# A gated cross-attention block on one core: seven block products folded onto one shared PSUM bank, and the row transposes of the feed-forward input spread over three attention units

## The reference

```
x  = x + tanh(g_xattn) * attention(layernorm(x), ctx)      # ctx: 8 x 750 x 1024
x  = x + tanh(g_ffn)   * ffn(layernorm(x))
attention: q = x Wq^T; k, v = ctx Wk^T, ctx Wv^T; 32 heads of 32; q and k rms-normalised;
           softmax(q k^T / sqrt(32)) v
ffn:       x1 = x Q(w1)^T; x2 = x Q(w2)^T; hidden = sigmoid(x1) * x2; out = hidden Q(w3)^T
Q(w):      clip(round(w / mean|w|), -1, 1)                 # 2816 x 1024, ternary
```

## Time and profile before

| what | value |
|---|---|
| three executions | 2386.88, 2387.74 (median), 2391.3 us |
| the profiled execution | 2394.38 us, its span 2392.6 us, mean granted clock 0.978 |
| busy, share of the span | PE 95%, PEld 55%, DVE 69%, ACT 60%, POOL 46% |
| one transpose into xT | 229 KB (112 rows of 1024 16-bit values; block 3 half of that) |
| one load of wraw | 2 transfers of 512 KB |

### The profile page before, as it was taken

How to read it: one execution, slowest core, us unless ns; L and a number is a source line. 1 busy time by engine, 2 the same in 40 slices (tenths; PEclk the granted TensorE clock), 3 DMA queues, 4 the chain that set the end, 5 groups by cost and what they waited for, 6 DMA issues and landing times.

```text
span 2392.6 us, 45650 instructions
## 1 busy us (share of the span) xinstructions
PE 2272.0 (95%) x16761; PEld 1313.5 (55%) x16786; DVE 1644.5 (69%) x2531; ACT 1427.2 (60%) x2931; POOL 1091.2 (46%) x993
## 2 busy tenths in 40 slices
PE   7998999999999999999999999878799999999999
PEld 6874566556656656556555566544344454444444
DVE  6776677786786877877877877677878666642220
ACT  5875788888888888888888888762222223221010
POOL 4674355674765756665765756642312222210000
PEclk9998999999999999999999999969899999999999
DMA  8885545545445546444545534668786454444331
GB/s 294 288 304 166 145 108 116 111 115 125 98 112 118 108 108 132 105 100 119 130 101 111 122 93 95 135 137 199 197 198 184 146 173 138 145 132 163 126 126 53
DMA packets 441328, 339.47 MB, mean 142 GB/s; under 512 B 366992, under 2 KB 388496, under 8 KB 440592
## 3 DMA queue, kind: packets, MB, share of 16 engines
q1 hardware_dynamic: 441104, 336.53, 53.9%
HBM read 184.68 MB, written 73.92 MB: 108 GB/s over the span
## 4 chain that ended last, share of the span: by engine, by line
POOL 35%; issue 28%; PE 21%; DMA 7%; DVE 6%; SPq 2%; ACT 1%; POOLq 0%; DVEq 0%; ACTq 0%
POOL krs L763 14%; PE ps L1682 11%; PE ps L1543 10%; DMA wraw<-in_wffn 5%; POOL oinv L781 5%; POOL kms L758 4%; POOL qrs L725 4%; DVE w12q L1277 2%; POOL osum L779 2%; DVE wneg L1275 2%; POOL osum L786 2%; SPq L487 1%; POOL oinv L783 1%; POOL ca L793 1%; DMA w12q<-w_ternary 1%
## 5 line engine op out<-in xcount | busy, mean ns | idle before, releaser
L1604 PE MATMUL ps<-wk,cpair 128*128 128x512 f16 x4608 | 1123.6, 381 | 18.4 <-DVE cpair L1190 10.6
L1394 DVE TENSOR_TENSOR plo<-pf,phi 125x448 f16<-125x448 f32 x768 | 570.6, 746 | 156.9 <-ACT phi L1029 154.7
L1604 PEld LDWEIGHTS ps<-wk,cpair 128*128 128x128 f16 x4608 | 395.2, 97 | 399.8 <-issue 14.1
L1038 ACT ACTIVATE pf<-ps 125x448 f32<-125x448 f32 x768 | 418.1, 544 | 141.8 <-PE ps L1624 135.3
L1029 ACT ACTIVATE phi<-pf 125x448 f16<-125x448 f32 x768 | 446.0, 581 | 8.9
L763 POOL TENSOR_TENSOR krs<-kms,mhalf 125x8 f32<-125x8 f32 x192 | 338.9, 1765 | 15.1
L758 POOL TENSOR_TENSOR kms<-kss,keps 125x8 f32<-125x8 f32 x192 | 95.3, 496 | 507.6 <-DVE kss L1360 507.6
L1648 PE MATMUL ps<-val,phi 125*128 125x65 f16 x3072 | 282.5, 193 | 41.2 <-DVE plo L1394 40.6
L1543 PE MATMUL ps<-xT,wT 128*128 128x448 f16 x1408 | 284.5, 356 | 14.3 <-DVE wT L1312 14.3
L1624 PEld LDWEIGHTS ps<-qT,kst 128*125 128x125 f16 x1536 | 212.1, 141 | 146.0 <-issue 1.8
L1624 PE MATMUL ps<-qT,kst 128*125 128x224 f16 x1536 | 280.6, 265 | 0.0
(11 more groups left out here) (120 smaller groups left out, 2848.8 us busy)
## 6 DMA issues: line engine op xcount, KB each, us to landing
gbuf<-in_wffn SPq DMA_DIRECT2D x66, 512.0 KB, 4.3
wraw<-in_wffn SPq DMA_DIRECT2D x66, 512.0 KB, 5.5
cstream<-in_ctx SPq DMA_DIRECT2D x48, 500.0 KB, 5.6
craw<-in_ctx SPq DMA_DIRECT2D x48, 500.0 KB, 4.5
hidden<-hf SPq DMA_DIRECT2D x88, 224.0 KB, 2.5
hraw<-hidden SPq DMA_DIRECT2D x14, 1408.0 KB, 6.5
q_stacked<-qnat SPq DMA_DIRECT2D x28, 512.0 KB, 3.6
w_ternary<-w12q SPq DMA_DIRECT2D x22, 512.0 KB, 3.0
```

What stands on the lines that cost most here:

```text
L1038: act.activation(pf[0:KW, e % 6, :], bank(3 + e % 3)[0:KW, 0:2 * S], ACT.Exp, bias=LN128, scale=SCALE).then_inc(p_ready, 1)
L1394: dve.tensor_tensor(plo[0:KW, e % 6, :, 0:S], pf[0:KW, e % 6, :].rearrange("p (t n) -> p t n", t=2), phi[0:KW, e % 6, :, 0:S], ALU.subtrac ...
L1604: mm = pe.matmul(bank(pt)[:, :], cpair[:, n % RING, a, kc, :], wkp[g][:, w, kc, :], start=(kc == 0 and m == 0), stop=(kc == KC - 1 and m = ...
```

## The change

Four groups of edits. (1) Phase C: the order of products becomes P1, P5, P6, P3, P7, P2, P4. P1, P6, P7 and P4 accumulate in bank 0, P5 and P3 in bank 1, P2 has bank 2. ScalarE copies the running sums out after P1, P5, P6 and P7 (`keep`: four instead of three), c21 is read by the second sigmoid straight from bank 0, c12 and c11 are the only additions of VectorE, and GpSimd makes c22 as one addition and the second half's gated product. (2) `wraw` gets a third slot; `load_w(n + 3)` stands first in SP's part of superpiece n, and `load_w(2)` right after the end of phase B. (3) 28 of the transposes into `xT` run in units 29 to 31, two or three behind each of four places in SP's order; the tail keeps the last four. Blocks 2 and 3 of a batch's rows are written in the first unit of batch b + 2 (before: in the last unit of batch b + 1), and saved there (`cn_save(4 * b - 6)`, `cn_save(4 * b - 5)`). (4) VectorE's wait for `q_saved` and the clearing of `knat` move behind the first `kss` sum.

```
         LN_STATS, LN_RSTD, LN_NORM = (4, 5), (5, 6), (6, 7)
-        LN_HIGH, LN_LOW = (6, 9, 13, 15), (7, 11, 14, 17)
-        LN_COMB = (8, 12)
+        LN_HIGH, LN_LOW = (6, 9, 18, 20), (7, 10, 19, 21)
+        LN_COMB = (8, 11)
...
-        def x_early(u, part):
-
-            if u == U - 1:
-                return {0: range(0, 4), 1: range(4, 8), 2: range(8, 12)}[part]
-            return range(12, 16) if u == U else ()
-
-        P1, P5, P7, P6, P2, P3, P4 = range(1, 8)
-        T1, T3, T2, T4 = range(1, 5)
+        X_EARLY = {U - 3: ((0, 0), (1, 0)), U - 2: ((2, 0), (3, 0), (0, 1)), U - 1: ((1, 1), (2, 1))}
+
+        def x_early(u, slot):
+
+            return [(4 * slot + q, part) for q, part in X_EARLY.get(u, ())]
+
+        P1, P5, P6, P3, P7, P2, P4 = range(1, 8)
+        T1, T2, T3, T4 = range(1, 5)
+        KEPT = ((P1, 0), (P5, 1), (P6, 0), (P7, 0))
...
-                s = j % 2
-                wait(sp, wquant_ready, 2 * (j - 1))
+                s = j % 3
+                wait(sp, wquant_ready, 2 * (j - 2))
...
                         turn_k(u - 1, 5)
+                        if u in X_EARLY:
+                            sp.wait_ge(kv_ready, KT * u)
+                        early_rows(u, 0)
...
-                        if g == G - 1 and b >= 1:
-                            cn_save(4 * b - 2)
-                        if u == U - 1:
-                            sp.wait_ge(kv_ready, KT * (U - 1))
-                        for ld in x_early(u, 0):
-                            turn_x(ld, (0, 1) if ld % 4 < 3 else (0,))
+                        early_rows(u, 1)
                         turn_k(u, 1)
-                        for ld in x_early(u, 1):
-                            turn_x(ld, (0, 1) if ld % 4 < 3 else (0,))
                         for m in gates_of_unit[1:-1]:
                             load_gates(m)
+                        early_rows(u, 2)
+                        if g == 0 and b >= 2:
+                            cn_save(4 * b - 6)
                         turn_k(u, 2)
                         load_gates(gates_of_unit[-1])
-                        for ld in x_early(u, 2):
-                            turn_x(ld, (0, 1) if ld % 4 < 3 else (0,))
+                        early_rows(u, 3)
                         if g == 1 and b >= 1:
                             x1_save(2 * b - 2)
                             x1_save(2 * b - 1)
                         turn_k(u, 3)
                         if g == 2 and b >= 1:
                             cn_save(4 * b - 3)
-                        if g == G - 1 and b >= 1:
-                            cn_save(4 * b - 1)
+                        if g == 0 and b >= 2:
+                            cn_save(4 * b - 5)
...
                     for bb in range(B // 2):
                         turn_x(4 * bb + 3, (1,))
                     load_w(1)
-                    for ld in x_early(U, 0):
-                        turn_x(ld, (0, 1) if ld % 4 < 3 else (0,))
+                    cn_save(4 * B - 6)
+                    cn_save(4 * B - 5)
...
             phase_b_over(sp)
+            load_w(2)
             x1_save(NL - 2)
             x1_save(NL - 1)
...
             for n in range(FJ):
+                if n + 3 < FJ:
+                    load_w(n + 3)
                 if n:
                     for half in range(2):
                         save_hid(n - 1, half)
                 if n + 1 < FJ:
                     save_w12(n + 1)
-                if n + 2 < FJ:
-                    load_w(n + 2)
                 if n - 1 in LATE_LOW:
                     cn_save(4 * B - 4 + LATE_LOW.index(n - 1))
                     later.append(4 * B - 4 + LATE_LOW.index(n - 1))
                 if later:
                     turn_x(later.pop(0))
...
-            def superpiece(n):
-
-                pool.wait_ge(prod_copied, 3 * n + 3)
-                wait(pool, c22_ready, n)
-                pool.tensor_tensor(s57[:, :], prod[:, n % 2, 1, :], prod[:, n % 2, 2, :], ALU.add).then_inc(s57_ready, 1)
-                pool.wait_ge(u2_ready, n + 1)
-                pool.wait_ge(s57_ready, n + 1)
-                wait(pool, hf_ready, 2 * n)
-                pool.tensor_tensor(c22[:, :], u2[:, n % 2, :], s57[:, :], ALU.add).then_inc(c22_ready, 1)
+            def gated(n):
+
+                pool.wait_ge(sg_ready[1], n + 1)
+                pool.wait_ge(c22_ready, n + 1)
+                pool.tensor_tensor(hf[:, n % 2, 1, :], hf[:, n % 2, 1, :], sg[:, 1, :], ALU.mult
+                                   ).then_inc(hf_ready[1], 1)
+
+            def sums(n):
+
+                pool.wait_ge(kept_ready, 4 * n + 4)
+                if n >= 2:
+                    pool.wait_ge(hid_saved[n % 2], 32 * (n // 2))
+                pool.tensor_tensor(hf[:, n % 2, 1, :], kept[:, n % 2, 3, :], kept[:, n % 2, 1, :], ALU.add
+                                   ).then_inc(c22_ready, 1)
...
             def gate(n, half):
 
-                b0 = 4 * (n % 2)
+                wait(act, hf_ready[half], n)
                 if half == 0:
-                    act.wait_ge(h_ready, product(n, P2))
-                    wait(act, hf_ready, 2 * n - 1)
+                    act.wait_ge(c11_ready, n + 1)
                 else:
-                    act.wait_ge(c21_ready, n + 1)
-                    wait(act, hf_ready, 2 * n)
-                act.activation(sg[:, half, :], bank(b0)[:, 0:CW] if half == 0 else c21[:, :], ACT.Sigmoid
-                               ).then_inc(sg_ready, 1)
+                    act.wait_ge(h_ready, product(n, P4))
+                act.activation(sg[:, half, :], c11[:, n % 2, :] if half == 0 else bank(4 * (n % 2))[:, 0:CW], ACT.Sigmoid
+                               ).then_inc(sg_ready[half], 1)
...
-            def keep_product(n, i):
-
-                act.wait_ge(h_ready, product(n, (P1, P5, P7)[i]))
+            def keep(n, i):
+
+                act.wait_ge(h_ready, product(n, KEPT[i][0]))
                 if n >= 2:
-                    act.wait_ge(u2_ready, n - 1)
-                    act.wait_ge(s57_ready, n - 1)
-                act.activation(prod[:, n % 2, i, :], bank(4 * (n % 2) + i)[:, 0:CW], ACT.Copy).then_inc(prod_copied, 1)
+                    act.wait_ge((c11_ready, c22_ready, c12_ready, c22_ready)[i], n - 1)
+                act.activation(kept[:, n % 2, i, :], bank(4 * (n % 2) + KEPT[i][1])[:, 0:CW], ACT.Copy).then_inc(kept_ready, 1)
 
             for n in range(NSP):
-                keep_product(n, 0)
-                keep_product(n, 1)
-                keep_product(n, 2)
-                gate(n, 0)
+                keep(n, 0)
+                if n:
+                    gate(n - 1, 0)
+                for i in range(1, 4):
+                    keep(n, i)
                 gate(n, 1)
                 if n in LATE_LOW:
                     ln_high(B - 1, LATE_LOW.index(n))
                 if n in EARLY_SPLIT:
                     hidden_high(0, EARLY_SPLIT.index(n))
+            gate(NSP - 1, 0)
...
             w_tables(0)
-            for c in range(2):
-                dve.wait_ge(q_saved[c], 16 * NT)
-            dve.memset(knat[:, :, :, :, :], 0.0).then_inc(knat_clear, 1)
+
+            def clear_knat():
+                for c in range(2):
+                    dve.wait_ge(q_saved[c], 16 * NT)
+                dve.memset(knat[:, :, :, :, :], 0.0).then_inc(knat_clear, 1)
...
                         dve.tensor_reduce(kss[0:KW, :], ksq[0:KW, :, :], AX_X, ALU.add).then_inc(kss_ready, 1)
+                        if Tb == 0:
+                            clear_knat()
...
+                dve.wait_ge(sg_ready[0], n + 1)
+                dve.wait_ge(c12_ready, n + 1)
+                dve.tensor_tensor(hf[:, n % 2, 0, :], hf[:, n % 2, 0, :], sg[:, 0, :], ALU.mult
+                                  ).then_inc(hf_ready[0], 1)
+
...
             for n in range(NSP):
-                b0 = 4 * (n % 2)
-                if n:
-                    second_half(n - 1)
                 if n + 1 < FJ:
                     quantise(n + 1, 0)
+                if n:
+                    gated(n - 1)
+                if n + 1 < FJ:
                     quantise(n + 1, 1)
                 if n >= FJ:
                     quantise_w3(n - FJ)
-                dve.wait_ge(h_ready, product(n, P6))
-                dve.wait_ge(prod_copied, 3 * n + 1)
-                if n >= 2:
-                    dve.wait_ge(c22_ready, n - 1)
...
+                wait(pe, sg_ready[1], n - 1)
                 block_product(n, 0, 0, w[:, 0, 0:4, :], True)
                 pe.wait_ge(t_ready, combo(n, T1))
                 wait(pe, c12_ready, n - 1)
                 block_product(n, 1, 2, t[:, 0, :, :], True)
-                pe.wait_ge(t_ready, combo(n, T3))
-                wait(pe, c21_ready, n - 1)
-                block_product(n, 2, 4, t[:, 1, :, :], True)
                 pe.wait_ge(t_ready, combo(n, T2))
-                wait(pe, u2_ready, n - 1)
-                block_product(n, 3, 6, t[:, 2, :, :], True)
```

(38 more changed lines are left out.)

59 lines of the change are left out of this document (27 added, 32 removed).

## The result

The changed kernel takes **2364.2 us** (median of 4 runs, 2360.1 to 2367.8) against 2387.3 (4 runs): ratio 0.990, 95% interval 0.988 to 0.992, 23 us less. Forecast were 2353.7 us and 34 less. The sign and the kind of gain held; a third of the gain is missing.

What follows compares the result with a forecast made beforehand. TensorE was taken to bound the attention, a load-quantise-save loop through a two-slot buffer the first pass. Terms -33 - 3 - 5.5 - 20 + 1.5 + 31 - 5 = -34 us gave 2353.7 us from 2387.7, range 2322 to 2374.

Steps and rivals of the forecast that it cites:

- first pass: First pass of gate and up products: third slot and earlier load end the wait for wraw; -33 us, to 246.
- second pass: Second pass of gate and up products: shorter first superpiece and smaller stalls after the early split; -3 us.
- start of the attention: Second context tile made before VectorE's wait and clearing, so TensorE gets it earlier; -5.5 us.
- blocks out of g = 3: Last unit of each batch: without GpSimd's low part holding VectorE up, 3.4 us go in six units; -20 us.
- crowding at the end of g = 2: Attention, end of units with g = 2: the moved first blocks crowd GpSimd; +1.5 us.
- new wait in g = 0: First unit of a batch: ScalarE waits 6 us for the cn save, TensorE 3.8 for plo; +31 us over six units.
- tail: Attention's tail: waits for kst go (-13.4), blocks (+1.6) and a save wait (+6) come; -5 us taken.
- Rival A: Attention, units with g = 0: the new wait costs nothing; -65 us, 2323 us; chance 0.13.
- Rival C: Units with g = 0: the wait leaves TensorE at half clock for ten steps; +33 us, 2421 us; chance 0.07.
- exclusive port: Skill's rule on VectorE and GpSimd: the stall moves with the block, making the -20 about 0; the forecast kept -20.
- Rival B: First pass: transfers bound it, 1.0 us more in each of sixteen superpieces; 2370 us; chance 0.14.
- Rival D: Nothing moves: a missed wait holds the first pass at 12.1 us, the attention cancels itself; 2388 us; chance 0.04.

Runs made afterwards that it cites:

- e1: Changed kernel with the save of block 2 ahead of the transpose of k tile 1 in units with g = 0; 2332.9 us, ratio 0.976 to before.
- e9: Kernel before with the third wraw slot, the earlier load and the second half's gated product on GpSimd; 2352.9 us, ratio 0.985 to before.
- e5: Kernel before with only the third wraw slot and the earlier load; 2365.8 us, ratio 0.991 to before.
- e4: Changed kernel with raw weights loaded as with two slots, behind the save of ternary weights; 2414.6 us, ratio 1.011 to before.
- e10: e8 with phase C's old order of products, banks and copies, keeping third slot and GpSimd's gated product; 2327.1 us, ratio 0.974 to before.
- e8: Changed kernel with block 2's save ahead in units and tail, last batch's blocks in superpieces 4, 6, 8, 10; 2318.4 us, ratio 0.971 to before.
- e12: Kernel before, unchanged, profiled once more; span 2385.9 us against 2392.6 in its first profile.

## Why the prediction was right, and what it mis-sized

The steps as measured, with the second profile of before beside the first where they differ:

| step | predicted | measured |
|---|---|---|
| first pass | -33, to 246 | -34.4 (-31.3), to 244.6 |
| of it late blocks, over 10.60 each | +7 | +8.0 (superpieces 5 to 8, P1 to P1: 10.59 + 15.80 + 13.03 + 10.99 - 4 x 10.60) |
| of it the queue of transfers | +3 | 0 (superpieces 9 to 20: 10.59 each) |
| second pass | -3 | -5.7 (-2.5) |
| start of the attention | -5.5 | -6.4 (-6.0) |
| blocks out of g = 3, with the crowding at the end of g = 2 | -20 + 1.5 | -16.2 together (estimate: -20.6 + 4.4) |
| new wait in g = 0 | +31 | +36.8 |
| unit 31 | 0 | +1.0 |
| tail | -5 | -3.7 (-4.3) |

**The new wait** was right in place, cause and length: ScalarE 5.7 to 7.0 us where 6 was said, TensorE 3.64 to 4.90 where 3.8 was said. Rival A is refuted by that, and e1 shows it by removal. Too small was the price of the clock: 1.4 us a unit, taken from rows 7, where the stall was 2.1 us. In units 8 to 28 TensorE waited 3.73, 3.66, 3.78, 3.77, 4.90 and 3.64 us for `plo` and was then at 0.50 for 5.4, 3.1, 5.3, 3.0, 4.1 and 6.0 us. The waits sum to 23.5 us, half of the time at 0.50 to 13.5, together 37.0 against the 36.8 that the intervals lost. The prediction had 6 x 3.8 = 22.8 and 6 x 1.4 = 8.4. Rival C's long half clock came in no unit.

**The blocks out of g = 3** gave 2.7 us by the intervals (44.47 to 41.76) and not 3.4, because a second term hides in them. At the end of unit 26 of the changed kernel, and alike in each of the intervals that end in units 7 to 27 with g = 3 and in unit 31:

```profile
1345.55 1.64 POOL L765 TENSOR_TENSOR krs<-kms,mhalf 125x8 f32<-125x8 f32 x1
...
1347.22 0.42 DVE L1387 SCALAR_TENSOR_TENSOR khat<-ps,krs 125x256 f32<-125x256 f32 x1 [3.18 <-POOL krs L765]
...
1347.71 1.47 PE L1614 MATMUL ps<-wk,cpair 128*128 128x512 f16 x6 [1.23 <-DVE khat L1387]
```

TensorE waits 1.23 us for `khat` (0.49 before the change), since GpSimd, which has the low part of block 1 there now (2.14 us from 1337.94) and the output sums behind it, comes late to `krs`. This is the crowding that the prediction put at +1.5 in all. The splitting of the next batch's tiles does not cause it: unit 3 has the splitting and no block, and its interval is 41.04; unit 31 has the block and no splitting, and takes 41.62 (40.63 before). So against 41.04 the blocks gave 3.4 us a unit, as forecast, and the crowding took 0.7 a unit, over 4 us in all; the division is an estimate from these intervals, and no run tried it.

The exclusive port was the Trainium skill's case against this gain ("SBUF — State Buffer", section "SBUF: two separate sides"). That an operation of VectorE takes longer beside one of GpSimd is in the traces (0.75 against 1.50 us in e9). That the stall would move with the blocks is not: they cost 2.7 us more in g = 3 than out of it, and in e1 499 - 495 = 4 us for six pairs, 0.65 each, in g = 0. In the interval of the kernel before that ends in unit 31, with the first of the two blocks and no splitting beside it, TensorE waits for nothing and takes 40.63 us. What such a slowing costs is what the engine held up has no slack for.

**The first pass** was sized right by reading the loop, but half of the reason stayed untested in the prediction. The slot alone gives 21 to 24 us. Another 10.6 lie between e5 and the changed kernel: 5 in the eleven superpieces at 11.04, 3 in the late blocks, 3 in the last superpiece. Those at 11.04 are VectorE's: with 10.0 us of work counted from rows 1, I had it at 8.8 after the change and left it there; e5 shows that at its old load it is the bound, because a wait of 0.64 us inside its own program comes on top of the work. And the new order is no gain by itself, but a dependence: with two slots it costs 15 to 18 us (e4), with three it is worth 3.7 in the first pass (e9 against changed) or 10.6 (e10 against e8), and costs 4 in the second. Phase C of e9, old order and all, takes 482.0 us, the changed kernel's 482.3.

**From the profile to the median.** Between the two profiled spans the change is 2363.5 - 2392.6 = -29 us. I made the sum against a profile that was 6.6 us over its median and then took it from the median. e12 places that excess in the two passes, where the change brings most superpieces down to TensorE's own 10.60; that it went with the loops it belonged to is read from two profiles, no more. Between typical executions (2385.9 and 2363.5) the difference is 22 us, as the medians say (23). So of 11 us missing in the gain, 5 to 6 were this, and the other 5 are g = 0 (+6), g = 3 with its crowding (+2), tail and unit 31 (+2), less 5 by which the passes and the start of the attention came out better.

Rival B is refuted by e8: engines at a full share beside a full TensorE. The 1.4 us that kept its chance alive was time on SP's queue, not shown to be time of the DMA engines; while those seven were issued (1550 to 1562) the engines stood at a share of 0.96 with 190 GB/s of all kinds of transfer. Rival D is refuted by the stages.

**The better version** is e8: the change with both saves ahead and the last blocks in every second superpiece, 2318.4 us, ratio 0.971 to before; by both ratios 0.981 to the changed kernel.

## What to carry to other kernels

When work is moved, read what its buffer waits for, and where in the in-order queue that release stands: here one line of SP's program was worth 31 us, more than the whole change (23). Before saying that an engine has room, add to its busy time the waits that its own program order forces on it. Where the profiled execution lies above the median, find the stage of the excess, best by a second profile, before a gain is taken from the median: here it lay in the two passes that the change shortened. A moment read once per unit mixes the end of one unit with the start of the next, and so can hide one term in another.

## What the runs showed that I had not expected

- The clock after a stall: 3.64 us of idle TensorE were followed by 6.0 us at 0.50 in unit 28, 3.66 us by 3.1 in unit 12 of the same program.
- One operation of 0.62 us moved off VectorE shortened a second pass in which VectorE was busy two thirds of the time (167 of 244 us) by 9.8 us (e5 to e9; the old order took 243.5 and 240.2 in its two profiles, so 3 us of this may be from run to run). TensorE's waits for the reload of ternary weights, 8.7 us in three pieces in e5, are down to under 2: the saves of the hidden rows, which stand ahead of the reload in SP's order, no longer wait for VectorE. That chain was not tried by itself.
